# Adjacency build of a graph kernel: POOL weighs the one-hots of 13 of 16 parts in one instruction, and VectorE makes these one-hots and all aim comparisons in broadcast form

## The reference, cut to what matters

```python
deg  = segment_sum(ew_f, dst_f, num_segments=n)
dis  = where(deg > 0, rsqrt(where(deg > 0, deg, 1.0)), 0.0)
norm = dis[src_f] * ew_f * dis[dst_f]
out  = segment_sum(h[src_f] * norm[:, None], dst_f, num_segments=n) + b
```

## Time and profile before

| | us |
|---|---|
| Median of 3 runs | 3844.22 (3842.1 to 3844.31) |
| The profiled execution, its own time | 3845.3 |
| Its span, first to last instruction | 3843.6 |
| Stage `adjacency`, first POOL comparison to the last | 154.5 to 737.1 |
| Busy over the whole span | PE 2980.3, DVE 2904.3, POOL 2197.2, ACT 2023.3 |

### The profile page before, as it was taken

One profiled execution on the slowest core, in us unless ns is written; L12 is line 12 of the kernel. 1 busy time (PEld: TensorE's weight loads), 2 busy tenths in 40 slices (PEclk: granted clock), 3 DMA queues, 4 the chain that ended last, 5 costly groups with the idle time before them and its releaser, 6 DMA issues. The chain is left out here.

```text
span 3843.6 us, 88662 instructions
## 1 busy us (share of the span) xinstructions
PE 2980.3 (78%) x17564; PEld 2375.2 (62%) x17565; DVE 2904.3 (76%) x8382; ACT 2023.3 (53%) x6416; POOL 2197.2 (57%) x2660
## 2 busy tenths in 40 slices
PE   4666676489999976677777877876588888888885
PEld 3466666478888863566666666654366666666663
DVE  6888888644443326899999999997687877788785
ACT  4133333234444415589899898884244444444444
POOL 3399999600000001777777777741577777777760
PEclk8889888899999988899999999998799999999997
DMA  3022222489999963777777777763487888888875
GB/s 100 12 71 65 66 65 72 94 250 267 265 269 301 290 154 110 201 226 229 228 226 227 222 228 223 223 174 88 131 225 223 224 228 222 227 229 225 226 208 139
DMA packets 396501, 716.25 MB, mean 186 GB/s; under 512 B 61376, under 2 KB 240222, under 8 KB 386870
## 3 DMA queue, kind: packets, MB, share of 16 engines
q1 hardware_dynamic: 315555, 494.95, 45.0%
q0 software_dynamic: 78992, 217.93, 21.4%
q10 hardware_dynamic: 1698, 0.85, 0.1%
HBM read 507.42 MB, written 206.06 MB: 186 GB/s over the span
## 5 line engine op out<-in xcount | busy, mean ns | idle before, releaser
L997 POOL DMA_INDIRECT rows<-table_d,idx x1612 | 1538.6, 954 | 507.4 <-issue 450.5
L2403 ACT ACTIVATE px<-rows,px 128x64 f32 (+1 forms) x4480 | 1266.3, 368 | 105.5 <-ACT px L2394 103.9
L2468 PE MATMUL psum<-px,ohf 128*128 128x264 f32 (+1 forms) x3648 | 952.1, 406 | 67.0 <-ACT px L2403 61.0
L2468 PEld LDWEIGHTS psum<-px,ohf 128*128 128x128 f32 x3648 | 680.3, 197 | 203.9 <-issue 45.9
L2419 PE MATMUL psum<-xr,ohT 125*128 x5472 | 707.7, 281 | 64.6 <-DMA ohT<-ohT_d 36.3
L2235 DVE TENSOR_TENSOR m<-rows,psum 128x1024 f32<-128x1024 f32 x456 | 554.0, 1215 | 240.0 <-POOLq L1013 135.5
L2419 PEld LDWEIGHTS psum<-xr,ohT 125*128 125x128 bf16 x5472 | 542.8, 100 | 205.3 <-issue 78.1
L1281 POOL TENSOR_SCALAR where<-aim,col_at 128x125 f32<-128x125 f32 x900 | 582.5, 666 | 0.1
L1329 PE MATMUL psum<-where,sw 128*125 128x125 f32 x2880 | 390.0, 302 | 189.4 <-POOL where L1281 153.5
L1329 PEld LDWEIGHTS psum<-where,sw 128*125 128x125 f32 x2880 | 375.3, 215 | 204.8 <-issue 204.8
L1294 DVE TENSOR_SCALAR sw<-iota,row_at,w_at 128x126 f32<-128x126 f32 x1440 | 417.9, 364 | 0.0
(11 more groups left out here) (419 smaller groups left out, 2916.6 us busy)
## 6 DMA issues: line engine op xcount, KB each, us to landing
ohf<-oh_d SPq DMA_DIRECT2D x456, 256.0 KB
adj_w<-adj_d SPq DMA_DIRECT2D x50, 1464.8 KB
oh_d<-ohfk SPq DMA_DIRECT2D x228, 256.0 KB, 9.3
ohT<-ohT_d SPq DMA_DIRECT2D x456, 128.0 KB
adj_d<-strip SPq DMA_DIRECT2D x25, 1464.8 KB
part_d<-part SPq DMA_DIRECT2D x228, 132.0 KB
part_d<-part SPq DMA_DIRECT2D x228, 129.0 KB
ohT_d<-ohTk SPq DMA_DIRECT2D x228, 128.0 KB, 7.7
```

The lines of the kernel that those rows point to most:

```text
L997: pool.indirect_dma_start(out=rows[0:n, s % RING, k, :], out_offset=None, in_=table, in_offset=bass.IndirectOffsetOnAxis(ap=idx[0:n, s // ...
L2403: last = nc.scalar.activation(px[:, i, k, h, 0:C], rows[:, bass.ds(r, 1), k, h * C:(h + 1) * C].squeeze(1), ACT.Copy, scale=px[:, i, k, h, ...
L2468: last = nc.tensor.matmul(psA[i], ohf[:, g.pos % FS, k, :], px[:, i, k].rearrange("p h c -> p (h c)"), start=k == 0, stop=k == K - 1)
```

## The change

POOL makes no `where` any more. DVE makes `where` of all 16 parts in one broadcast `tensor_tensor` (2000 elements). `sw` of the first 13 parts is now made in two instructions on two engines: DVE writes the bare one-hots (is_equal of `iota` with `row_at`, both in broadcast form, 13 x 126 = 1638 elements) into a new tile `hot`, and POOL multiplies that by the weights, repeated over 126 elements, in one `tensor_tensor` into `sw`. `sw` of the last 3 parts is made as before, by 3 `tensor_scalar` on DVE. POOL now waits for DVE in each step (`s_hot`), DVE waits for POOL's product of 3 steps ago before it overwrites `hot` (`s_swp`), and PE waits for `s_swp` where it waited for POOL's `where`.

```diff
-POOLED = 10
+POOLED = 13
@@ adjacency
+            hot = sb("row_hot", [P, DEEP, POOLED, WN + 1], F32, st)
-            def place(s, lo, hi):
-                n = hi - lo
-                return nc.vector.tensor_tensor(where[:, s % DEEP, lo:hi, :], aim[:].unsqueeze(1).to_broadcast([P, n, MC]),
-                                               col_at[:, s * STEP + lo:s * STEP + hi].unsqueeze(2).to_broadcast([P, n, MC]), ALU.is_equal)
+            def spread(tile, s, n, width):
+
+                return tile[:, s * STEP:s * STEP + n].unsqueeze(2).to_broadcast([P, n, width])
@@ gpsimd
-                        for i in range(POOLED):
-                            p = s * STEP + i
-                            last = nc.gpsimd.tensor_scalar(where[:, s % DEEP, i, :], aim[:], col_at[:, p:p + 1], None, ALU.is_equal)
-                        last.then_inc(s_wherep, 1)
+                        pool.wait_ge(s_hot, s + 1)
+                        nc.gpsimd.tensor_tensor(sw[:, s % DEEP, 0:POOLED, :], hot[:, s % DEEP], spread(w_at, s, POOLED, WN + 1),
+                                                ALU.mult).then_inc(s_swp, 1)
@@ vector
                             dve.wait_ge(s_mm, STEP * (s - DEEP + 1))
-                        place(s, POOLED, STEP).then_inc(s_where, 1)
-                        for i in range(STEP):
+                            dve.wait_ge(s_swp, s - DEEP + 1)
+                        V.tensor_tensor(hot[:, s % DEEP], iota[:, 0:WN + 1].unsqueeze(1).to_broadcast([P, POOLED, WN + 1]),
+                                        spread(row_at, s, POOLED, WN + 1), ALU.is_equal).then_inc(s_hot, 1)
+                        V.tensor_tensor(where[:, s % DEEP], aim[:].unsqueeze(1).to_broadcast([P, STEP, MC]),
+                                        spread(col_at, s, STEP, MC), ALU.is_equal).then_inc(s_where, 1)
+                        for i in range(POOLED, STEP):
@@ tensor, put
-                        pe.wait_ge(s_wherep, g.count())
+                        pe.wait_ge(s_swp, g.count())
```

More of the change, by code:

```diff
@@ L1240, in adjacency @@
             sw = sb("sw", [P, DEEP, STEP, WN + 1], F32, st)
+            hot = sb("row_hot", [P, DEEP, POOLED, WN + 1], F32, st)
             strip = sb("strip", [P, 2, NWIN, WN], F32, st)
-            s_set, s_where, s_wherep, s_sw, s_mm, s_free, s_strip = (sem("adj_" + n) for n in (
-                "set", "where_made", "where_made_pool", "sw_made", "summed", "slots_free", "strip_taken"))
+            s_set, s_where, s_hot, s_swp, s_sw, s_mm, s_free, s_strip = (sem("adj_" + n) for n in (
+                "set", "where_made", "hot_made", "sw_made_pool", "sw_made", "summed", "slots_free", "strip_taken"))
             s_out = [sem(f"adj_out{i}") for i in range(2)]
```

## The result

| | us |
|---|---|
| Kernel before, median of 4 runs on this chip | 3843.16 (3837.27 to 3844.31) |
| Changed kernel, median of 4 runs | 3916.17 (3913.94 to 3919.76) |
| Ratio | 1.0197, 95% interval 1.0185 to 1.0209 |
| Profiled execution: its own time, its span | 3913.94, 3912.2 |

The change makes the kernel slower by 73.0 us between the medians (1.90%); 3931 was forecast, with a range from 3885 to 4030. Between the two profiled executions the distance is 68.6 us.

A forecast was written before the change was run, and what follows sets the result against it. POOL alone was taken to bound the adjacency stage, 6.47 us per step. The change's 1.77 + 2.15 + 2.73 + 0.78 = 7.43 us over 90 steps gave 669 against 582.5 us, +86: about 3931 us, range 3885 to 4030.

The forecast's parts named there:

- product's hold on DVE: Adjacency stage, each step: POOL's product of 1638 elements holds DVE for 2.73 us, at 1.66 ns per element.
- the row of the attention layer: Attention layer's POOL product, 1280 elements, one input repeated: holds DVE for 2.13 us; the forecast's product was priced from it.
- small delays: Adjacency stage: DVE's `tensor_scalar` delayed by about 0.06 us whenever a POOL comparison of 125 elements gets in.
- The rival that had them hidden: Adjacency stage: three `tensor_scalar` run beside POOL's product; step 6.65 us, +16, total 3861 us; chance 0.06, partly hidden included.
- The dearer product: Adjacency stage: product's hold 3.84 us, step 8.54 us, +186, total 4031 us; chance 0.10 for 3965 to 4035.
- the dense row: POOL's dense product of 896 elements in 2.10 us: 2.34 ns per element, 3.84 us for 1638 if all is held.
- The broadcast row: POOL product of 1280 elements with one input repeated, holding DVE 2.13 us: 1.66 ns per element, 2.73 us for 1638.
- 3956: Adjacency stage: total with the product at 3.0 us, +111 us; counted to the forecast.
- the stage's tail: End of the adjacency stage: one PE step, the last copy and the last store; claimed the same in both kernels.
- the clock's rival: Adjacency stage: PE at its lower clock, 1.2 GHz, needs 7.5 us per step; +6 us, within the range; no separate chance.
- The rival on the faster side: Adjacency stage: no exclusion for these forms, DVE bounds at 4.70 us per step; -160, total 3685 us; chance 0.08.

## Why the prediction was right

**The bound and the mechanism.** The argument was that a two-input DVE instruction and a POOL instruction that reads SBUF take turns, and that therefore the step becomes the sum `hot` + `where` + product + 3 `tensor_scalar`. The trace shows the sum, and the two experiments with the wait taken away (7.35 us) and the reading taken away (5.17 us) show that it is POOL's reading and not its new wait. POOL's product showed 4.79 us where 4.9 were forecast, and PE waited for DVE's or POOL's `sw` in 78 of the 90 steps, "nearly every" one.

**The terms.** Forecast and measured, in us per step:

| | forecast | measured | from |
|---|---|---|---|
| `hot` | 1.77 | 1.78 | 307.68 to 309.46 |
| `where` | 2.15 | 2.15 | 309.46 to 311.61 |
| product's hold on DVE | 2.73 | 2.61 | 2949 - 335 ns |
| 3 `tensor_scalar` | 0.78 | 0.77 | 3.38 from 311.61 to 314.99, less 2.61 |
| step | 7.43 | 7.31 | |

The one term that was off is the product: 0.12 us, 11 us of the stage's 90 steps. It was scaled from 1280 to 1638 elements in proportion. The rate of 1.66 ns was right (1.67 between the two sizes measured), but the line through these two has a fixed part of -0.12 us and gives 2.02 us for 1280 elements, where the row of the attention layer had 2.13. There the held instruction was a `tensor_tensor`, here it is a `tensor_scalar`; whether that makes the difference isn't shown.

**The `tensor_scalar`.** I counted them as shut out on the strength of small delays. That is what the first of each three shows at 2.94 us. The rival that had them hidden (3861 us) is out. The small delays didn't show this much by themselves: they come from comparisons that held DVE for 0.06 us each, and that a long product shuts the `tensor_scalar` out for nearly its whole length was an inference that came true.

**The dearer product.** 4031 us by the dense row, or about 4005 us by the page of the Trainium skill ("GPSIMD Engine Reference", "Elementwise — side-by-side cycle accounting"). Measured: the whole product takes 2.92 us where nothing stands before it, against the page's estimated 3.55. The broadcast row was the one to go by the earlier trace rows.

**Readings and sums.** Three small things in the prediction don't hold, and none moves its result. POOL's digits are nines in five slices (2 to 6, counted from 0), and slice 7 has a 6. The 900 comparisons were split into 0.57 us each and 0.77 us for each held one, which was read from a single one; over the whole trace a comparison starts 0.577 us after the one before, 1.28 us where it is held, so the hold is 0.70 us on average and the split 519 + 63 us. And the rivals' 4031, 3956, 4005 and 3861 us are counted from the profiled execution, without the 1.1 us that the forecast takes off.

**The tail and the rest.** As forecast, the stage's tail is unchanged, the next stage starts 74.2 us later, and PE waits mostly for DVE's `sw` (155.2 us, then POOL's 46.5). PE's granted clock went from 0.89 to 0.84 in the stage, and PE's busy time from 390.0 to 431.7 us, without touching the chain: the clock's rival cost nothing, and DVE never waited for PE. Of the forecast +86 us, 75 came in the stage (the 0.12 us per step) and 73.0 in the medians.

**What was missing.** The rival on the faster side was priced at 4.70 us per step by DVE alone. The run without the product gives 5.72: I had PE at 4.33 us by its busy time alone and took no account of the stretches in which it stands idle, whose cause stays open. This did not touch the forecast, but it would have made the fast case 90 us too low.

## What to carry to other kernels

Before work goes from a busy engine to a less busy one, ask what the two share: here the broadcast forms made the work planned for each engine look smaller, and the sum of their holds on SBUF became the step. Look in the trace for one instruction of each kind that lies under the other, and read how much longer it takes; that number, times the count, is the price. POOL helps beside DVE with many short one-input operations (0.58 us each, of which DVE feels 0.06); one large operation that reads SBUF holds DVE for almost its whole length, the one-input copy for 1.24 of 1.41 us as well as the two-input product for 2.61 of 2.78.

## What else the runs showed of the hardware

A POOL memset, which reads nothing, leaves DVE's two-input instructions alone but holds its `tensor_scalar` of 126 elements: 0.46 us in each step. And a register load of 16 words from SBUF by PE takes 1.10 us at best and up to 5.35 us at worst, one of 8 words 0.59 to 3.21 us. In the kernel without the product nearly all of PE's long idle stretches, 2.5 to 5.4 us each, lie over the slow ones.
